# A graph network's GRU on one core: the tile of 53 rows taken last instead of ninth

## The chip, the cores and the metric

The kernel runs on 1 core of one Trainium2 chip. The metric is device time in microseconds of one execution. The median of the three runs of the kernel before is 858.27 us (856.66 to 858.71). Engine names are those of the profile: PE is TensorE (PEld its weight loads), DVE is VectorE, ACT is ScalarE, POOL is GpSimd, and SPq is the queue on which SyncE issues transfers.

## The reference, cut to what matters

3125 nodes have 256 features each; 103125 edges (with loops) join them. A layer norm and three graph convolutions come first and give `x` anew. The second half is one relational step whose result goes through a GRU cell, node by node:

```python
h = jnp.maximum(_layernorm(x, axis=-1), 0.0)
msg = h[edge_src] + relvectors[edge_rel]
red = jax.ops.segment_sum(msg, edge_dst, num_segments=h.shape[0])
gi = red @ w_ih.T + b_ih              # 3125 x 768
gh = h @ w_hh.T + b_hh
r = sigmoid(i_r + h_r); z = sigmoid(i_z + h_z)
n = tanh(i_n + r * h_n)
x = x + (1.0 - z) * n + z * h
```

## The kernel before, in words

The nodes are cut into T = 25 tiles of 128 rows, of which the last, tile 24 (`T - 1`), holds only 53 (`TAIL`). The edges are turned once into a matrix of counts, `count`, which stays on chip, so that every sum over neighbours is a row of dense f16 matmuls. All engines' programs are written by hand, instruction by instruction, and joined by semaphores; nothing reorders them. What an engine executes, and in which order, is the order of the Python calls.

The last stage is the relational sum with the GRU. The sum for the 24 full tiles is made in three parts, p = 0, 1 and 2, of eight tiles each (tiles 0 to 7, 8 to 15, 16 to 23), by a scheme with seven products in place of eight for each part. The sum for tile 24 is made apart, by `rest_pe` during p = 0, and is kept in `rest_sum`, a place in SBUF of its own, until the GRU takes it. While PE makes the products of part p, it puts the GRU of the eight or nine tiles of part p - 1 between them; the GRU of part 2 stands after all products. `gru_order` says which tile the GRU takes as its nth, and `gru_before(p)` how many tiles it takes before those of part p. The tail of PE's program for one part reads, in `paired_sums_next_pe` (n is `gru_before(p - 1)`):

```python
            product_pe(p, T3, every, False, nothing).then_inc(product_done, 1)
            for g in range(n + 6, gru_before(p) - 1):
                gru_pe(g)
            last_tail_pe(p)
            gru_pe(gru_before(p) - 1)
```

`product_pe` is line L1744 of the profile and `last_tail_pe` two matmuls at L1752. DVE's program has the same form: it adds up the blocks of a sum (`block_dve`, L1898) between its tiles of the GRU.

One tile of the GRU is, on PE (`gru_tile_pe`): input to the r and z gates (L757), state to the r and z gates (L764), state to the n gate (L769), input to the n gate (L774), all in f32 with 256 features in two halves. DVE and ACT follow (`gru_tile_dve`, L790 to L809; `gru_tile_act`, L706 to L735): bias, sigmoid, tanh, and the mix with the state and the residual. L790 waits for the matmuls of L764, and L809 makes the result.

The transposed state of a tile, which the matmuls of L764 and L769 take as stationary operand, is read from DRAM (`state_scratch`) into one of two places. SP issues these loads, the stores of the results and the loads of `x1` in one queue:

```python
            if stored and i + 2 < T:
                SP.wait_ge(nh_done, i + 1)
                state_load_sp(order, i + 2)
            SP.wait_ge(result, i + 1)
            SP.dma_start(out[t * P:t * P + rows(t), :], ...)
            if i + AHEAD < T:
                gru_load_sp(order, i + AHEAD)
```

A full tile's state takes 4 transfers of 32 KB (L664), the short one's takes 8 of 8 KB. `nh_done` is counted when L769 of the tile is through, so the state of a tile is asked for when the tile two before it has let go of the place. The store of a result is L692, the load of `x1` L668.

Of the kernel before, what the change touches and what calls it, by code (L numbers as in the profile page):

```python
# [53 lines left out]
def program(nc, x, src, dst, rel, convs, relvec, w_ih_t, w_hh_t, b_ih, b_hh, x1_dram, table_dram, mixed_dram, second_dram, h_dram, out):  # L54
# [3 lines left out]
    T = -(-N // P)  # L58
# [24 lines left out]
    with ExitStack() as ctx:  # L83
# [1347 lines left out]
        def layers_pe():  # L1431
# [42 lines left out]
            for n in range(gru_before(2), T):  # L1474
                gru_pe(n)
# [7 lines left out]

        gru_order = [*range(0, 8), T - 1, *range(8, T - 1)]
        first_sum, rest_sum = far_stage.rearrange("p c a d -> p (c a d)").bitcast(F32), pair_b[:, 0:2, :]
        block_sums = [(agg[:, 0, :], agg[:, 1, :], *(weight[f].rearrange("p f d -> p (f d)") for f in range(2))),
                      tuple(block_sums_b)]
# [1 line left out]

        def gru_before(p):

            return 8 * p + 1 if p else 0

        def columns_of(p, half):
            return slice(p * FREED + half * CHUNK, p * FREED + (half + 1) * CHUNK)
# [322 lines left out]
        def paired_sums_next_pe(p):  # L1820

            n, every = gru_before(p - 1), range(PAIRED)
            if p > 1:
                PE.wait_ge(*block_out_at(p - 1, "c21"))
# [28 lines left out]
            for g in range(n + 6, gru_before(p) - 1):  # L1853
                gru_pe(g)
# [778 lines left out]
```

## Time and profile before

| | us |
|---|---|
| median of three runs | 858.27 |
| the profiled execution's own time | 857.42 |
| its span | 853.2 |
| PE busy in the span | 821.6 (96%) |
| DVE busy | 606.7 (71%) |
| ACT busy | 297.6 (35%) |

The span is from the first to the last recorded event of the execution; its own time is 4.22 us more. A term of a sum is made against 857.42. The GRU's tiles run from 658 us to the end.

### The profile page before, as it was taken

To read this page: it belongs to the slowest core of one execution; us is meant where nothing else is said; L and a number is where in the kernel's file an instruction comes from. 1 tells how busy PE (TensorE), PEld (TensorE's weight loads), DVE (VectorE), ACT (ScalarE), POOL (GpSimd) and SP (SyncE) were. 2 spreads that over 40 slices of the span, in tenths; PEclk is the share of its full clock that TensorE was granted. 3 is DMA by queue.
4 is the path that set the end of the run, shared out by engine and by line. 5 is a ranking of instruction groups with operands and counts; after the bars stand their busy time and mean duration, and the time that the engine had idled before them with its cause. 6 is when DMAs were issued, how large, how long until landed. Compare 5 with 4: busy or idle time off the path is not lost.

```text
span 853.2 us, 14286 instructions
## 1 busy us (share of the span) xinstructions
PE 821.6 (96%) x4710; PEld 465.7 (55%) x4710; DVE 606.7 (71%) x1319; ACT 297.6 (35%) x604; POOL 123.8 (15%) x244
## 2 busy tenths in 40 slices
PE   2889999999999999999999999999999999999997
PEld 1457566666666545445555544555554555455554
DVE  8955999999999265555867546575665656565677
ACT  3365666776777312110101302221202122112233
POOL 0210112013000036655760000000000000000000
PEclk9989999999999999999999999999999999999999
DMA  6100000000000511613301112222704112112232
GB/s 208 33 2 1 4 18 23 16 17 18 24 17 17 171 30 51 183 41 76 76 8 49 59 50 98 87 75 84 201 23 145 38 42 51 28 37 44 56 81 52
DMA packets 89689, 49.83 MB, mean 58 GB/s; under 512 B 52843, under 2 KB 86396, under 8 KB 89612
## 3 DMA queue, kind: packets, MB, share of 16 engines
q1 hardware_dynamic: 73836, 39.00, 16.3%
q10 hardware_dynamic: 15776, 9.85, 4.1%
q8 instruction: 42, 0.69, 0.3%
q14 instruction: 35, 0.29, 0.1%
HBM read 29.68 MB, written 18.78 MB: 57 GB/s over the span
## 4 chain that ended last, share of the span: by engine, by line
PE 89%; DVE 7%; issue 1%; ACT 1%; DMA 1%; SPq 0%; DVEq 0%
PE ps L1396 19%; PE ps L1058 13%; PE ps L1744 11%; PE ps L955 9%; PE ps L1570 9%; PE ps L757 5%; PE ps L764 5%; PE ps L1421 4%; PE ps L1439 3%; PE ps L769 2%; PE ps L774 2%; PE ps L1030 2%; PE ps L986 1%; DVE node_b L298 1%; PE ps L1018 1%
## 5 line engine op out<-in xcount | busy, mean ns | idle before, releaser
L1058 PE MATMUL ps<-node_a,count 128*128 128x512 f16 x525 | 181.0, 381 | 1.5 <-DVE node_a L1165 1.1
L955 PE MATMUL ps<-node_b 128*128 128x175 f16 x808 | 162.2, 256 | 5.5 <-DVE node_b L298 3.5
L298 DVE TENSOR_TENSOR node_b<-node_b 128x1024 f16<-128x1024 f16 (+2 forms) x253 | 157.1, 669 | 0.0
L1254 ACT ACTIVATE count<-ps 128x500 f32 x202 | 122.9, 608 | 65.1 <-PE ps L955 59.4
L1396 PE MATMUL ps<-count,node_a 128*128 128x512 f16 (+2 forms) x686 | 130.7, 351 | 0.0
L2329 POOL TENSOR_TENSOR count<-count,node_a 16x20 f16 x202 | 89.7, 444 | 94.9 <-DMA chapter_starts<-in_dst 53.9
L955 PEld LDWEIGHTS ps<-node_b 128*128 128x128 f16 x808 | 79.5, 100 | 35.0 <-issue 7.0
L1396 PEld LDWEIGHTS ps<-count,node_a 128*128 128x128 f16 (+1 forms) x686 | 60.1, 98 | 69.1 <-issue 0.4
L1744 PE MATMUL ps<-count,node_a 128*128 128x512 f16 x288 | 64.1, 379 | 0.0
L1058 PEld LDWEIGHTS ps<-node_a,count 128*128 128x128 f16 x525 | 53.2, 101 | 18.9 <-ACT count L1254 1.2
L727 ACT ACTIVATE count<-count 128x512 f32<-128x512 f32 (+1 forms) x25 | 15.8, 630 | 118.3 <-DVE count L790 118.3
L1570 PE MATMUL ps<-count,node_b 128*128 128x512 f16 x240 | 52.9, 379 | 0.7 <-issue 0.7
L1069 POOL TENSOR_TENSOR count<-count,ident 128x128 f16<-128x128 f16 x21 | 24.2, 1151 | 185.5 <-ACT count L1254 185.5
L1702 DVE TENSOR_TENSOR count<-count 128x6144 f16<-128x6144 f16 x14 | 47.0, 3355 | 5.0 <-PE ps L1570 4.4
L1744 PE MATMUL ps<-count,node_b 128*128 128x512 f16 x216 | 47.6, 379 | 0.1
L764 PE MATMUL ps<-count,node_b 128*128 128x512 f32 (+1 forms) x100 | 47.0, 592 | 0.0
L1396 PE MATMUL ps<-count,node_b 128*128 128x512 f16 (+3 forms) x300 | 46.2, 314 | 0.0
L1744 PEld LDWEIGHTS ps<-count,node_a 128*128 128x128 f16 x288 | 28.1, 98 | 33.0
L2115 ACT ACTIVATE agg<-ps,scales 128x512 f32<-128x512 f32 (+1 forms) x20 | 12.1, 608 | 86.2 <-PE ps L1421 52.1
L790 DVE TENSOR_TENSOR count<-ps,count 128x512 f32<-128x512 f32 (+1 forms) x25 | 17.3, 691 | 32.7 <-PE ps L764 32.6
L1570 PEld LDWEIGHTS ps<-count,node_b 128*128 128x128 f16 x240 | 23.4, 98 | 28.9 <-issue 1.1
L966 PE MATMUL ps<-node_b 128*128 128x25 f16 x201 | 38.9, 194 | 0.0
(289 smaller groups left out, 1134.0 us busy)
## 6 DMA issues: line engine op xcount, KB each, us to landing
node_a<-in_x SPq DMA_DIRECT2D x4, 768.0 KB, 8.2
second_scratch<-node_a ACTq DMA_DIRECT2D x4, 768.0 KB, 3.8
node_a<-second_scratch ACTq DMA_DIRECT2D x4, 768.0 KB, 4.3
node_b<-second_scratch ACTq DMA_DIRECT2D x8, 384.0 KB, 5.1
state_scratch<-params SPq DMA_DIRECT2D x24, 128.0 KB, 1.9
node_b<-state_scratch SPq DMA_DIRECT2D x96, 32.0 KB, 2.1
table_scratch<-agg SPq DMA_DIRECT2D x21, 128.0 KB, 1.8
mixed_scratch<-node_b SPq DMA_DIRECT2D x10, 256.0 KB, 2.0
```

The costliest lines, as they stand in the source:

```text
L298: return DVE.tensor_tensor(to, iota, keys.unsqueeze(2).to_broadcast([P, n, width, 2]), ALU.is_equal)
L757: PE.matmul(ps[0:m, rz, 0:2 * D], sums[f], w_ih_rz[:, f, :], start=(f == 0), stop=False)
L764: done = PE.matmul(ps[0:m, rz, 0:2 * D], hs[f], w_hh_rz[:, f, :], start=False, stop=(f == HALVES - 1))
L955: return PE.matmul(window(s)[:, :, keys], low, key_hot[k][:, j, :, i].rearrange("p (t w) -> p t w", w=SPAN), start=(s == 0 and j == 0), st ...
L966: PE.matmul(window(s + 1)[:, :, 0], low, carry_hot[s // GROUP % 2][:, s % GROUP // 2, :, i], start=True, stop=False, skip_group_check=True)
L1058: last = PE.matmul(out_slot(u)[0:m, :], count[:, t, u * P:u * P + m], node_a[:, t, :, :].rearrange("p a d -> p (a d)"), start=(t == 0), st ...
L1254: ACTE.activation(to, window(s), ACT.Copy).then_inc(win_written, 1)
L1396: done = PE.matmul(ps[:, b, 0:cols], nodes[0:k, t, part, f * P:(f + 1) * P], count[0:k, t, c * CHUNK:c * CHUNK + cols], start=(first and n ...
L1570: done = PE.matmul(to, second_table(p, which, i, part), count[:, 2 * i + odd, columns_of(p, half)], start=(start and i == 0 and part == 0) ...
L1702: DVE.tensor_tensor(to, to, of, op).then_inc(step_made, 1)
L1744: done = PE.matmul(ps[:, bank_of(p, which), :], table_of(which, i, part), count[:, 2 * i + odd, columns_of(p, half)], start=(start and n = ...
L2329: POOL.tensor_tensor(to, to, chapter_counts[chapter % 2][:, at_place // GROUP, at_place % GROUP, :], ALU.add).then_inc(rel_placed, 1)
```

## The change

The GRU takes the tiles in plain order, 0 to 24. The short tile, until now the ninth (after tiles 0 to 7, and so at the end of the products of part 1), becomes the twenty-fifth and last, and the GRU has 8, 8 and 9 tiles after parts 0, 1 and 2 where it had 9, 8 and 8. No work is added or removed: each engine has as many instructions as before.

```diff
-        gru_order = [*range(0, 8), T - 1, *range(8, T - 1)]
+        gru_order = [*range(T)]
...
         def gru_before(p):
 
-            return 8 * p + 1 if p else 0
+            return 8 * p
```

On PE this is how the end of the products of part 1 reads before the change. The first two rows end the GRU of tile 7, L1752 is `last_tail_pe(1)`, the rows with 53 are the short tile, and L1744 are the first 72 matmuls of part 2.

```order
L774 MATMUL ps<-count,params 128x256
L774 MATMUL ps<-count,agg 128x256
L1752 MATMUL ps<-count,node_b 128x512 x2
L757 MATMUL ps<-count,node_b 53x512 x2
L764 MATMUL ps<-count,node_b 53x512 x2
L769 MATMUL ps<-count,node_b 53x256 x2
L774 MATMUL ps<-count,node_b 53x256 x2
L1744 MATMUL ps<-count,node_b 128x512 x72
```

And this is the same place on PE with the change; the rows between L1752 and L1744 are now tile 7.

```order
L1752 MATMUL ps<-count,node_b 128x512 x2
L757 MATMUL ps<-count,params 128x512
L757 MATMUL ps<-count,agg 128x512
L764 MATMUL ps<-count,node_b 128x512 x2
L769 MATMUL ps<-count,node_b 128x256 x2
L774 MATMUL ps<-count,params 128x256
L774 MATMUL ps<-count,agg 128x256
L1744 MATMUL ps<-count,node_b 128x512 x72
```

The short tile has left this place, and `last_tail_pe(1)` stands one tile of the GRU nearer to the products of T3 that are ahead of it, as it does in part 2 in both kernels.

On SP's queue the kernel's last transfers before the change are these (state of tile 23, result of tile 21, then the last two results):

```order
L692 DMA out<-pair_a 128x256
L668 DMA xt<-x_scratch 128x256
L664 DMA node_b<-state_scratch 32x8x32 x4
L692 DMA out<-pair_a 128x256
L692 DMA out<-count 128x256
L692 DMA out<-pair_a 128x256
L2526 UNCONDITIONAL_BRANCH
```

With the change the same seven rows, where tile 24 is the last, read so:

```order
L692 DMA out<-pair_a 128x256
L668 DMA xt<-x_scratch 53x256
L664 DMA node_b<-state_scratch 32x2x32 x8
L692 DMA out<-pair_a 128x256
L692 DMA out<-count 128x256
L692 DMA out<-pair_a 53x256
L2526 UNCONDITIONAL_BRANCH
```

The last result is one of 53 rows, and the last load of a state is one of 8 transfers where it was one of 4.

## Rows read from the trace of the kernel before

**Rows 1.** The page's head and its first line of busy times.
```profile
span 853.2 us, 14286 instructions
PE 821.6 (96%) x4710; PEld 465.7 (55%) x4710; DVE 606.7 (71%) x1319; ACT 297.6 (35%) x604; POOL 123.8 (15%) x244
```

**Rows 2.** Three stretches: us; busy PE, PEld, DVE, ACT, POOL; clock, DMA share, GB/s.
```profile
658.44:727.57 69.13, 69.13 (x249) 36.31 (x247) 43.82 (x84) 16.52 (x34) 0.00 (x0) 1.00 0.19 44
727.57:801.71 74.14, 74.14 (x290) 38.61 (x290) 41.55 (x74) 14.55 (x30) 0.00 (x0) 1.00 0.16 37
801.71:848.16 46.45, 46.45 (x145) 27.16 (x143) 35.46 (x82) 16.85 (x35) 0.00 (x0) 1.00 0.29 69
```

**Rows 3.** Timeline of PE around the short tile: start us, us, instruction.
```profile
721.75 0.60 PE L1752 MATMUL ps<-count,node_b 112*128 112x512 f16 x2
722.27 1.92 PE L757 MATMUL ps<-count,node_b 128*53 128x512 f32 x4
724.03 1.88 PE L764 MATMUL ps<-count,node_b 128*53 128x512 f32 x4
...
727.57 15.71 PE L1744 MATMUL ps<-count,node_b 128*128 128x512 f16 x72
```

**Rows 4.** Timeline of PE, a full tile between the same two neighbours.
```profile
743.12 0.60 PE L1752 MATMUL ps<-count,node_b 112*128 112x512 f16 x2
...
748.72 5.34 PE L1744 MATMUL ps<-count,node_a 128*128 128x512 f16 x24
```

**Rows 5.** Timeline of PE, the last two tiles.
```profile
837.83 1.02 PE L757 MATMUL ps<-count,params 128*128 128x512 f32 x2
...
842.99 1.02 PE L757 MATMUL ps<-count,params 128*128 128x512 f32 x2
...
844.70 1.88 PE L764 MATMUL ps<-count,node_b 128*128 128x512 f32 x4
```

**Rows 6.** Timeline of DVE and SP's queue after the last full tile.
```profile
846.62 0.69 DVE L790 TENSOR_TENSOR count<-ps,count 128x512 f32<-128x512 f32 x1 [0.77 <-PE ps L764]
...
850.58 0.42 DVE L809 TENSOR_TENSOR pair_a<-pair_a 128x256 f32<-128x256 f32 x1
851.03 0.33 SPq L692 DMA_DIRECT2D out<-pair_a  x1
```

**Rows 7.** The same timeline after the short tile.
```profile
725.95 0.68 DVE L790 TENSOR_TENSOR count<-ps,count 53x512 f32<-53x512 f32 x1 [0.68 <-PE ps L764]
...
729.87 0.42 DVE L809 TENSOR_TENSOR count<-count,pair_a 53x256 f32<-53x256 f32 x1
730.31 0.28 SPq L692 DMA_DIRECT2D out<-count  x1
```

**Rows 8.** The same for the stretch of the last store.
```profile
851.80:852.40 0.60, 0.00 (x0) 0.00 (x0) 0.00 (x0) 0.00 (x0) 0.00 (x0) 0.50 0.65 213
```

**Rows 9.** Transfers: the last store, then all 25 stores (L692), issue to landing.
```profile
out<-pair_a SPq DMA_DIRECT2D x1, 128.0 KB, 2.1
...
DMA to landing us min/median/max: 1.7/1.7/3.2
```

**Rows 10.** Loads of states on SP's queue: the short tile's, and the last full one's.
```profile
715.92 3.61 SPq L664 DMA_DIRECT2D node_b<-state_scratch  x8
...
837.16 2.53 SPq L664 DMA_DIRECT2D node_b<-state_scratch  x4
```

**Rows 11.** Landing of these: the short tile's eight, then all 104 of L664.
```profile
node_b<-state_scratch SPq DMA_DIRECT2D x8, 8.0 KB, 1.6
...
L664 SPq DMA_DIRECT2D node_b<-state_scratch x104: 325/612/1089, 644.3 to 839.1; - x104
...
DMA to landing us min/median/max: 1.5/2.1/4.4
```

**Rows 12.** Timeline of part 2's end: block sum after T3, then last_tail_pe.
```profile
796.31 0.75 DVE L1898 SCALAR_TENSOR_TENSOR params<-ps,scales,node_b 128x512 f32<-128x512 f32 x1 [2.53 <-PE ps L1744]
...
801.27 0.60 PE L1752 MATMUL ps<-count,node_b 112*128 112x512 f16 x2
```

## The prediction

> **What bounds the kernel now.** I read the page first: PE is busy for 821.6 of 853.2 us [rows 1]. That is a mean over the whole kernel, so I then asked for the busy times of the stretches in which the GRU runs. From the first tile of the GRU to the end of the last one PE is busy in every one of the 69.13, 74.14 and 46.45 us, at a granted clock of 1.00, which is the upper of its two levels (2.4 GHz). DVE is busy for 43.82, 41.55 and 35.46 us of the same stretches and ACT for 16.85 at most [rows 2]. So from 658.44 to 848.16 us the time is PE's work, and it does not matter in which order PE does it, unless an order makes PE wait. What is not PE's work stands behind it: after the last matmuls of L764 DVE and ACT still have the whole of a tile's gates to do, and then the result is stored. This drain begins at 846.62 and ends with the span at 853.2 [rows 1, 6], 6.58 us. The change can act in three ways only: on what the short tile costs PE, on the drain, and by a new wait.
>
> The sum is made against the profiled execution: span 853.2, own time 857.42, so 4.22 us lie outside the span. The median of the runs shown is 858.27, 0.85 us above it.
>
> **PE's part.** The short tile has 53 columns of stationary operand in place of 128, but its moving operands are as wide as a full tile's. From the start of `last_tail_pe(1)` ahead of it to the first product behind it are 727.57 - 721.75 = 5.82 us [rows 3]. The same piece with a full tile in it takes 748.72 - 743.12 = 5.60 us [rows 4]. So the short tile is no cheaper for PE than a full one; it costs 0.22 us more, in two places. A full tile takes 842.99 - 837.83 = 5.16 us [rows 5], so `last_tail_pe` ahead of it takes 5.60 - 5.16 = 0.44. The short tile's L757 begins 722.27 - 721.75 = 0.52 after it, 0.08 later than that, and goes on to L764 in 724.03 - 722.27 = 1.76 us, where the last full tile takes 844.70 - 842.99 = 1.71 [rows 3, 5], 0.05 more. The other 0.09 us lie at the end, where PE returns to 128 columns. These look like weight loads that are not hidden where the shape changes. Put last, the short tile still pays the first two (0.13), since they stand ahead of its L764, and not the third, since no matmul of 128 columns follows. This term is **-0.09 us**.
>
> All else on PE only changes place. Between `last_tail_pe(1)` and the products of part 2 stands a full tile now, 7, as in part 2 it does before. Everything from there on to the end of tile 23 comes 5.16 + 0.22 = 5.38 us earlier, and the last tile gives back 5.16 + 0.13 = 5.29, which is the -0.09 again.
>
> **The drain, DVE and ACT.** From the start of L790 to the issue of the store are 851.03 - 846.62 = 4.41 us for the last full tile [rows 6] and 730.31 - 725.95 = 4.36 us for the short one [rows 7]. Fewer partitions make these instructions no shorter: L790 takes 0.69 on 128 rows and 0.68 on 53. The term is **-0.05 us**.
>
> **The last store.** Issued at 851.03, it lands 2.1 us later [rows 6, 9], and the span ends 2.17 us after the issue. In the stretch from 851.80 to 852.40 the chip moves 213 GB/s for 0.60 us, which is 128 KB, the store itself [rows 8]. At that rate the 53 KB of the short tile take 54272 / 213e9 = 0.25 us in place of 131072 / 213e9 = 0.62, so 0.36 us less. This is an upper bound for an orderly case, since the first and the last bytes do not come at that rate; the lower bound is nothing, for the other stores of 128 KB land in 1.7 us in the median [rows 9], which shows that 0.4 us of a landing can come and go for reasons other than size. Together, 0.36 and that 0.4 bound it from above at 0.8. I take **-0.30 us**, near what the rate gives, since the last store has no other traffic beside it.
>
> The Trainium skill, on its page "DMA: Bandwidth & Descriptors", section "Anatomy of one DMA", puts a transfer at a fixed part of about 2.0 us, most of it the receipt of the write, and a variable part of its bytes over 436 GB/s. By that rule the 75 KB less are worth an estimated 0.18 us, and the whole sum would be 0.32 us where mine is 0.44. The trace agrees that most of the 2.1 us do not depend on the bytes (0.60 us of it moves them), but not with a constant, since other stores of the same size landed in 1.7.
>
> **What the change moves on SP.** The short tile's state is loaded with 8 transfers, 3.61 us of SP's queue, where a full tile's 4 take 2.53 [rows 10]. Now they are the last load, asked for when L769 of tile 22 is through. Before, the last load started at 837.16 and the matmuls of L764 that want it at 844.70: 7.54 us, and 7.67 with the 0.13 above. 3.61 of issue and 1.6 of landing [rows 10, 11] are 5.21, which leaves 2.46 us. Behind these transfers in SP's queue waits the store of tile 22, for which nobody waits, and the two last stores come 5 and 10 us later. They were asked for in just this rhythm of full tiles before, at 715.92, and PE took the short tile with none but the 0.08 us of delay. This edit costs nothing, and up to the 2.46 us it stays so.
>
> **What is moved on DVE and ACT at the end of part 1.** `last_tail_pe(1)` waits for the block sum of T3 on DVE. It stood two tiles of PE's work behind T3, and now one. In part 2 it stood one tile behind already: the block sum starts at 796.31, takes 0.75, and `last_tail_pe` starts at 801.27 [rows 12], so 4.21 us of cover are left. The block sum c22 (L1898, 0.75 us each) now stands ahead of tile 7 rather than of the short tile; it is the order of part 2. This costs nothing; without the cover it would be 0.75 us once.
>
> **Sum.** -0.09 - 0.05 - 0.30 = -0.44 us, so 857.42 - 0.44 = 856.98 for an execution like the profiled one, and 858.27 - 0.44 = 857.83 beside the median. A new measurement is a median too, and I forecast **857.8**.
>
> **The rivals.**
>
> A late state, slower. Mechanism: the 8 transfers of the last state, in the densest part of the GRU, land after PE wants them, and PE waits at L764 of the last tile, with nothing behind it to fill the gap. It decides once issue and landing take over 7.67 us. With the longest landing of the trace, 4.4 us [rows 11], they take 3.61 + 4.4 = 8.01, 0.34 late, still not to be measured. If all eight issues took the longest 1.09 us too [rows 11], they would take 8 x 1.09 + 4.4 = 13.12, 5.45 late, and the time would be 857.83 + 5.45 = 863.3. For it speaks a DMA share of 0.29 there against 0.19 in the first stretch [rows 2]; against it, that the same eight took 3.61 and 1.6 before. Chance 3%.
>
> A drain that shrinks with the rows, faster. If a tile of 53 rows went through the gates in 53/128 of the time, 4.41 x 75/128 = 2.58 us would go, and 2.97 with the 0.30 of the store and the 0.09 of PE, so 858.27 - 2.97 = 855.3. The rows of the two tiles, 4.41 and 4.36 us, are against it [rows 6, 7]. Chance 1%.
>
> No gain at the store. Its landing is the round trip, and a store that is shorter ends no sooner: 858.27 - 0.14 = 858.1. For it speaks the spread between 1.7 and 2.1 at one size. Chance 20%. By the skill's rule above it would be an estimated 857.95, between this and the forecast.
>
> My forecast has 73%; 3% are left for what I have not seen, such as another wait at the end of part 1, on either side.
>
> **How the numbers follow.** The three runs before lie between 856.66 and 858.71, so about 0.3% (2.6 us) is what a measurement can tell from no change. All of my sum, and its bounds from -0.14 to -0.94, lie well within that. The range takes the lowest run with the largest gain, 856.66 - 0.94 = 855.7, made 856.0 since both at once are unlikely in a median, and reaches up to 859.8: the highest run without a gain, 858.71 - 0.14 = 858.6, and about as much again as the runs differ from their median (0.4 to 1.6), for a chip on another day. Faster by over 0.3%: 3% (the shrinking drain, half of the unseen, chance of the measurement); slower: 4% (the late state, and the rest); within: 93%.
>
> **What would show it.** In the profile after: PE busy without idle time from the first tile to the last; L1744 of part 2 starting about 5.4 us sooner than 727.57; the last L790 on 53 rows starting at 846.53; 4.36 us from there to the last store, and less than 2.17 from that to the end; a span near 852.8. I am wrong if PE idles ahead of the last L764, if the last load of a state takes over 7 us, or if `last_tail_pe(1)` waits for DVE.

## The result

The changed kernel takes 859.84 us in the median of 11 runs (858.52 to 860.68), the kernel before 857.63 (856.56 to 858.71) beside it. The ratio is 1.0025, with a 95% interval from 1.0017 to 1.0033, so the change makes it slower by 1.5 to 2.8 us. The forecast was 857.8 with a range from 856.0 to 859.8. The direction was wrong, and the time lies just outside the range.

The profiled execution of the changed kernel took 858.70 us with a span of 854.7, against 857.42 and 853.2 before. These are the stretches of the GRU that answer to [rows 2], columns as there:

```profile
658.64:721.95 63.31, 63.31 (x232) 34.22 (x231) 39.84 (x75) 14.46 (x30) 0.00 (x0) 1.00 0.19 44
721.95:796.07 74.12, 74.12 (x290) 38.60 (x289) 41.70 (x74) 14.64 (x30) 0.00 (x0) 1.00 0.16 38
796.07:847.82 51.75, 51.75 (x161) 29.16 (x159) 39.37 (x91) 18.92 (x39) 0.00 (x0) 1.00 0.29 67
```

PE is busy throughout, at the full clock, as before. One tile has moved from the first stretch to the last. Nothing inside the GRU was lost. The timeline of PE around the last tiles, to be held against [rows 3, 5]:

```profile
721.51 0.59 PE L774 MATMUL ps<-count,agg 128*128 128x256 f32 x2
721.95 15.70 PE L1744 MATMUL ps<-count,node_b 128*128 128x512 f16 x72
...
837.35 1.02 PE L757 MATMUL ps<-count,params 128*128 128x512 f32 x2
...
842.60 1.92 PE L757 MATMUL ps<-count,node_b 128*53 128x512 f32 x4
844.36 1.88 PE L764 MATMUL ps<-count,node_b 128*53 128x512 f32 x4
```

Part 2 starts at 721.95 where it was 727.57. From the L757 of tile 23 to that of the short tile behind it are 842.60 - 837.35 = 5.25 us, and from there to its L764 844.36 - 842.60 = 1.76, against 5.16 and 1.71 with a full tile in the last place. What follows is the drain, the timeline of DVE and of SP's queue that answers to [rows 6, 7]:

```profile
846.28 0.68 DVE L790 TENSOR_TENSOR count<-ps,count 53x512 f32<-53x512 f32 x1 [0.91 <-PE ps L764]
...
850.19 0.42 DVE L809 TENSOR_TENSOR pair_a<-pair_a 53x256 f32<-53x256 f32 x1
850.63 0.26 SPq L692 DMA_DIRECT2D out<-pair_a  x1
```

The last store is issued at 850.63, 0.40 us earlier than before. But the span ends at 854.7, 4.07 us after that issue, where it was 2.17: with a last store of 53 KB the end comes 1.9 us later than with one of 128 KB. The windows after the issue (columns as in [rows 8]) say how:

```profile
851.60:853.80 2.20, 0.00 (x0) 0.00 (x0) 0.00 (x0) 0.00 (x0) 0.00 (x0) 0.50 0.08 21
853.80:854.70 0.90, 0.00 (x0) 0.00 (x0) 0.00 (x0) 0.00 (x0) 0.00 (x0) 0.50 0.07 22
```

The 128 KB moved at 213 GB/s with 0.65 of the 16 DMA engines busy [rows 8]. The 53 KB move at 21 to 22 GB/s with a share of 0.07 to 0.08, and one engine of 16 is 0.0625. The little above it belongs to another queue (q14): the view of transfers from 851.60 to 853.80 gives the queue of the store (columns: packets, MB, share of the 16 engines)

```profile
q1 hardware_dynamic: 38, 0.04, 6.3%
```

It looks as if one engine writes all rows, one after another.

The differences add up to the span's. From the first L757 of the GRU (658.64, before 658.88) to the last L790 it is 187.64 us against 187.74, -0.10; from there to the store 4.35 against 4.41, -0.06; from the store to the end 4.07 against 2.17, +1.90. That is +1.74 us, and the GRU began 0.24 earlier in this execution, which leaves +1.5. The +1.74 lies in the interval of the timed runs, 1.5 to 2.8. The medians differ by more, 2.2 us; the last section shows why.

### The profile page after: what moved, and what is told of

Read it like the earlier page. It is cut to its first block, busy times and chain, and to the rows that moved or that the text cites. A ratio compares the mean times of both kernels' runs of the same rounds, so it can differ in the third digit from the quotient of the medians.

```text
span 854.7 us, 14286 instructions
## 1 busy us (share of the span) xinstructions
PE 820.6 (96%) x4710; PEld 465.0 (54%) x4710; DVE 606.6 (71%) x1319; ACT 297.4 (35%) x604; POOL 121.9 (14%) x244
## 4 chain that ended last, share of the span: by engine, by line
PE 89%; DVE 7%; issue 1%; ACT 1%; DMA 1%; SPq 0%; DVEq 0%
PE ps L1396 19%; PE ps L1058 13%; PE ps L1744 11%; PE ps L955 9%; PE ps L1570 9%; PE ps L757 5%; PE ps L764 5%; PE ps L1421 4%; PE ps L1439 3%; PE ps L774 2%; PE ps L769 2%; PE ps L1030 2%; PE ps L986 1%; DVE node_b L298 1%; PE ps L998 1%
## 5 line engine op out<-in xcount | busy, mean ns | idle before, releaser
L1744 PE MATMUL ps<-count,node_a 128*128 128x512 f16 x288 | 64.1, 379 | 0.0
L1069 POOL TENSOR_TENSOR count<-count,ident 128x128 f16<-128x128 f16 x21 | 21.9, 1045 | 187.6 <-ACT count L1254 187.6
L1744 PE MATMUL ps<-count,node_b 128*128 128x512 f16 x216 | 47.6, 379 | 0.1
L764 PE MATMUL ps<-count,node_b 128*128 128x512 f32 (+1 forms) x100 | 47.0, 592 | 0.0
L1744 PEld LDWEIGHTS ps<-count,node_a 128*128 128x128 f16 x288 | 28.1, 98 | 33.1
L790 DVE TENSOR_TENSOR count<-ps,count 128x512 f32<-128x512 f32 (+1 forms) x25 | 17.3, 690 | 32.7 <-PE ps L764 32.6
```

Of the source, the lines that this page charges most:

```text
L764: done = PE.matmul(ps[0:m, rz, 0:2 * D], hs[f], w_hh_rz[:, f, :], start=False, stop=(f == HALVES - 1))
L1744: done = PE.matmul(ps[:, bank_of(p, which), :], table_of(which, i, part), count[:, 2 * i + odd, columns_of(p, half)], start=(start and n = ...
```

## The experiments

The theory of the first four was the one engine; the rivals were the place of the short tile with the new division into 8, 8 and 9 tiles, and a last store that lands late whatever its form.

**The last store in 48 and 5 rows.** On top of the changed kernel:

```diff
-            SP.dma_start(out[t * P:t * P + rows(t), :], h_tile[slot][0:rows(t), :]).then_inc(out_done[slot], 16)
+            cuts = (0, 48, 53) if stored and i == T - 1 else (0, rows(t))
+            for r0, r1 in zip(cuts, cuts[1:]):
+                SP.dma_start(out[t * P + r0:t * P + r1, :], h_tile[slot][r0:r1, :]).then_inc(out_done[slot], 16)
...
```

The lines left out make SP's wait at the end count one store more, here and wherever a store is cut below.

> The changed kernel with its last store, 53 rows, cut into one of 48 rows and one of 5. Theory: a store's rows are dealt over the 16 DMA engines only where their number has a common factor with it that allows it; 53 is prime, so one engine writes all 53 rows one after another, about 2.87 us / 53 = 54 ns each. Cut, the 48 go 3 to an engine and the 5 take 0.27 us, after 0.35 us of a second issue: from the first issue to the end of the span 1.8 to 2.2 us in place of 4.07, so the time 1.9 to 2.3 us below the changed kernel's and within 0.5 of the kernel before (ratio 0.9995 to 1.0003). Rival 1, the place of the short tile or the new division of 8, 8 and 9 tiles costs the time: the ratio stays at 1.0025. Rival 2, a last store lands late whatever its size or form: from its issue to the end stays 4 us.

It took 857.13 us, ratio to the kernel before 1.0005 (0.9996 to 1.0015). SP's queue at its end:

```profile
850.75 0.71 SPq L694 DMA_DIRECT2D out<-pair_a  x2
```

The span is 853.0, so 2.25 us from the first issue to the end in place of 4.07. As far as can be measured the whole loss is gone with this one edit, with the order of the change left as it is. Place and division are not the cause, and a last store is not late as such.

**The short tile second last.** On top of the changed kernel:

```diff
-        gru_order = [*range(T)]
+        gru_order = [*range(T - 2), T - 1, T - 2]
```

> The changed kernel with the short tile second last (tiles 0 to 22, 24, 23), so 8, 8 and 9 tiles as in the change, and a last store of 128 rows. Theory of the one engine: the short store's slow landing is covered by the last tile's 5.16 us, the end is that of the kernel before: last store to end 2.17 us, ratio 1.0000 within 0.0005. Rival 1, place or division costs: ratio 1.0020 to 1.0025.

It took 858.35 us, ratio 1.0010 (1.0001 to 1.0019). That is above what I expected, though the interval takes in my upper bound of 1.0005. Its profiled execution took 856.96 us with a span of 853.1, and SP's queue reads:

```profile
845.61 0.28 SPq L692 DMA_DIRECT2D out<-count  x1
851.01 0.34 SPq L692 DMA_DIRECT2D out<-pair_a  x1
```

The last store is issued at 851.01 (before: 851.03) and the end is 2.1 us later. The profile thus shows an end like that of the kernel before; the short store, issued at 845.61, has 7.5 us. Most of the 0.1% in the timed runs goes with the granted clock: 6 of its 11 executions had a mean clock of 0.991, and 7 of the 27 of the kernel before. At 0.991 the medians are 858.65 and 858.30, at 0.995 (3 and 14 executions) 856.96 and 856.72. What is left, 0.2 to 0.4 us, is not explained.

**127 rows and 1 in the kernel before.** The last store, of 128 rows, with `cuts = (0, 127, 128)`.

> The kernel before with its last store, 128 rows, cut into one of 127 rows and one of 1. Theory of the one engine: 127 is prime too, so 127 rows run on one engine, 127 x 54 ns = 6.9 us, and from the first issue to the end are 1.2 + 6.9 + 0.05 = 8.1 us in place of 2.17: slower by 5.9 us, ratio 1.0069. Rival 1 (place or division): no more than a second issue, 0.3 us, ratio 1.0004. Rival 2 (whatever comes last lands late): the same, 1.0004.

It took 862.55 us in four executions, ratio 1.0059 (1.0043 to 1.0074). SP's queue, and the window of the transfer:

```profile
851.60 1.60 SPq L694 DMA_DIRECT2D out<-pair_a  x2
```

```profile
853.00:858.00 5.00, 0.00 (x0) 0.00 (x0) 0.00 (x0) 0.00 (x0) 0.00 (x0) 0.50 0.08 25
```

The span is 859.0: 7.4 us from issue to end, with the same share of 0.08 at 25 GB/s (6.7% of it the queue of the store). The single row waited behind the 127: these 5 us hold only packets of 1 KB, and the two short packets that belong to the two stores come behind them, from 858.0 to 858.5 (the short packets are explained with the table below). A loss of this kind appears in the old order, with a full tile, once the rows of the store are 127. It is smaller than the 8.1 us forecast, since my 54 ns a row were too many. From 53 rows in 4.07 us and 128 rows in 7.4 follow (7.4 - 4.07) / 75 = 44 ns for each row of 1 KB, 23 GB/s, and 4.07 - 53 x 0.044 = 1.7 us that do not depend on the rows.

**51 rows and 2.** The changed kernel with `cuts = (0, 51, 53)`.

> The changed kernel with its last store cut into 51 rows and 2. If the number of engines is the largest divisor of the rows up to 16, 51 = 3 x 17 rows go to 3 engines, 17 x 54 ns = 0.92 us: from the first issue to the end about 2.1 to 2.3 us, some 1.9 below the changed kernel. If only multiples of 16 are dealt out and all else goes to one engine, 51 x 54 ns = 2.75 us and 3.95 to 4.1 us to the end, the same as the changed kernel (ratio 1.0025).

It took 857.47 us, ratio 1.0003 (0.9994 to 1.0012). Queue and window:

```profile
851.01 0.60 SPq L694 DMA_DIRECT2D out<-pair_a  x2
```

```profile
851.80:852.60 0.80, 0.00 (x0) 0.00 (x0) 0.00 (x0) 0.00 (x0) 0.00 (x0) 0.50 0.19 51
```

The span is 853.4, so 2.39 us to the end. The DMA share is 0.19, which is three engines of 16 (0.1875). 17 rows each make 1.7 + 17 x 0.044 = 2.45. So it is not that only multiples of 16 are dealt out: 51 rows, which 3 divides, go over three engines.

**120 rows and 8 in the kernel before.** `cuts = (0, 120, 128)`, the same number of stores as with 127 and 1.

> The kernel before with its last store, 128 rows, cut into one of 120 rows and one of 8: two stores, as with 127 and 1. If the number of engines is the largest divisor of the rows up to 16, 120 rows go to 15 engines, 8 each, and the 8 rows to 8 engines, 0.34 us later: first issue to end 2.1 to 2.4 us, ratio 1.0000 within 0.0008. If only multiples of 16 are dealt out, 120 rows run on one engine, and 1.68 + 120 x 0.045 = 7.1 us are needed, ratio 1.0057. It also prices the cut itself, which the run with 127 and 1 had in it.

It took 857.49 us, ratio 1.0002 (0.9993 to 1.0012). The queue and the window:

```profile
851.21 0.70 SPq L694 DMA_DIRECT2D out<-pair_a  x2
```

```profile
852.00:852.60 0.60, 0.00 (x0) 0.00 (x0) 0.00 (x0) 0.00 (x0) 0.00 (x0) 0.50 0.77 201
```

The span is 853.5, 2.29 us to the end, at 201 GB/s. A cut costs 0.1 us here (2.29 against 2.17), and 120 rows, no multiple of 16, are not slow.

**The load of the short tile's x1 in 48 and 5 rows.** Its store is left alone:

```diff
-            SP.dma_start(x1_tile[i % AHEAD][0:rows(t), :], x1_dram[t * P:t * P + rows(t), :]).then_inc(x1_in[i % AHEAD], 16)
+            cuts = (0, 48, 53) if order is gru_order and t == T - 1 else (0, rows(t))
+            for r0, r1 in zip(cuts, cuts[1:]):
+                SP.dma_start(x1_tile[i % AHEAD][r0:r1, :], x1_dram[t * P + r0:t * P + r1, :]).then_inc(x1_in[i % AHEAD], 16)
...
```

The part left out is ACT's wait for x1, which counts one transfer more.

> The changed kernel with the load of the short tile's x1 (53 rows, L668) cut into 48 and 5, the store left alone. Theory of the one engine: ACT's L706 of the short tile waited 0.98 us for this load in the changed kernel; cut, it lands 2 us sooner and that wait is gone, but since L727 behind it still had 1.06 us of idle time, the time stays that of the changed kernel: ratio 1.0025, last store to end 4.0 to 4.1 us. Rival: the load is what costs the 2 us, ratio 1.0000.

It took 858.73 us, ratio 1.0016 (1.0007 to 1.0025), in which interval both the changed kernel's 1.0025 and the +1.74 us of its trace (1.0020) lie, and 1.0000 does not. Its median is 1.1 us below the changed kernel's, but not at a like clock: at 0.994 its six executions took 858.5 to 858.8 us and the changed kernel's three 858.5 to 858.7. In the changed kernel the timeline of ACT showed a wait for this load:

```profile
838.65 0.42 ACT L735 ACTIVATE pair_a<-pair_a 128x256 f32<-128x256 f32 x1 [1.03 <-DVE pair_a L800]
840.05 0.60 ACT L706 ACTIVATE pair_a<-xt,negmr,rstd 53x256 f32<-53x256 f32 x1 [0.98 <-DMA xt<-x_scratch]
841.71 0.63 ACT L727 ACTIVATE count<-count 128x512 f32<-128x512 f32 x1 [1.06 <-DVE count L790]
```

With the load cut, where L706 has become L708 and L735 L737, and SP's last store stands under them:

```profile
839.94 0.42 ACT L737 ACTIVATE pair_a<-pair_a 128x256 f32<-128x256 f32 x1 [1.03 <-DVE pair_a L802]
840.26 0.59 ACT L708 ACTIVATE pair_a<-xt,negmr,rstd 53x256 f32<-53x256 f32 x1
```

```profile
851.91 0.26 SPq L694 DMA_DIRECT2D out<-pair_a  x1
```

The wait is gone, and the end still comes 4.1 us after the store (span 856.0). In the changed kernel the load was issued at 835.47 and ACT could start 4.58 us later, where the landings of L668 that the view gives have a median of 2.1. That fits one engine for the load too; its engines were not read apart, since the state's transfers ran beside it. The load was 1.06 us from costing something: that much idle time stood behind it on ACT.

**52 rows by SP and 1 by ACT.** The changed kernel with a last store of 52 rows, and at the end of ACT's program:

```diff
+            ACTE.wait_ge(result, T)
+            ACTE.dma_start(out[N - 1:N, :], h_tile[(T - 1) % AHEAD][TAIL - 1:TAIL, :]).then_inc(out_done[(T - 1) % AHEAD], 16)
```

> The changed kernel with its last store in two that are issued at once: 52 rows by SP (52 = 4 x 13, so 13 engines with 4 rows each) and the last row by ACT, which is through by then. First issue to end 1.68 + 4 x 0.045 = 1.9 us, where the cut into 48 and 5 on SP alone took 2.25, and the chain ahead of it is 0.14 us shorter than in the kernel before: 0.4 us below the kernel before, ratio 0.9995, too little to be told from 1. Should ACT's issue be slower than SP's, it ends like the cut into 48 and 5.

It took 857.55 us, ratio 1.0001 (0.9992 to 1.0010). Both transfers are issued together:

```profile
852.01 0.34 SPq L694 DMA_DIRECT2D out<-pair_a  x1
852.01 0.49 ACTq L2198 DMA_DIRECT2D out<-pair_a  x1
```

The span is 854.0, so 2.0 us from issue to end, the shortest of all and 0.2 below the kernel before. In the time it can't be told from the kernel before, as expected. No version tried beats it by what can be measured.

## Why the prediction was wrong

**The step that failed** is "The last store": the term of -0.30 us measured +1.90. I took the rate of a transfer of 128 rows, 213 GB/s, and let 53 rows run at it, as if only the bytes counted. The runs show that the number of rows decides over how many engines they are dealt: 53 and 127 over one, 51 over three, 120 and 128 over about all.

The traces hold a count that says the same without any rate. Each row is a packet of 1 KB, and some packets under 512 B come with every store. Here is the line of packets from the last store on, for 53 rows, for 48 and 5, and for 51 and 2 (packets under 2 KB are the 53 rows and the short ones):

```profile
DMA packets 57, 0.08 MB, mean 19 GB/s; under 512 B 1, under 2 KB 54, under 8 KB 54
DMA packets 80, 0.10 MB, mean 10 GB/s; under 512 B 21, under 2 KB 74, under 8 KB 74
DMA packets 64, 0.10 MB, mean 10 GB/s; under 512 B 5, under 2 KB 58, under 8 KB 58
```

These are 1, 21 and 5 short packets, and the largest divisors up to 16 are 1 for 53, 16 + 5 for 48 and 5, and 3 + 2 for 51 and 2. In all seven cases of the table below the count is that sum. So the 5 rows went over five engines, where my expectation for that run had put them on one.

The ends go by 1.7 us and 44 ns for each row of the busiest engine, to within 0.2 us (a second issue on SP comes 0.35 us after the first):

| last store | short packets | rows on the busiest engine | 1.7 + rows x 0.044 | issue to end, us |
|---|---|---|---|---|
| 128 rows (before) | 16 | 8 | 2.05 | 2.17 |
| 53 rows (changed) | 1 | 53 | 4.03 | 4.07 |
| 48, then 5 | 21 | 3, then 1 | 2.09 with 0.35 | 2.25 |
| 51, then 2 | 5 | 17 | 2.45 | 2.39 |
| 127, then 1 | 2 | 128 | 7.33 | 7.4 |
| 120, then 8 | 23 | 8, then 1 | 2.09 with 0.35 | 2.29 |
| 52 and 1 at once | 14 | 4 | 1.88 | 2.0 |

The cases of 53 and of 127 rows fixed the two numbers; the other five did not. The 0.16 and 0.2 us of the two stores with 0.35 in their sum are not explained. That these are numbers of engines is read from the share of busy time, the divisors and the short packets; no row names an engine.

The Trainium skill has the rule, on the same page that the prediction drew on ("DMA: Bandwidth & Descriptors"), in the section "Why a DMA increments its semaphore by 16 and not by 1": a transfer is split over the largest number up to 16 that divides the outermost dimension of both its sides, and 127 rows get one engine. The traces agree in every case above (for 53: 22 GB/s where 128 rows had 213). That page of the Trainium skill gives the rule of 2.0 us and 436 GB/s, which the prediction held beside its own term, for transfers issued by GpSimd; this store is issued by SP. By that rule 53 KB would land in an estimated 2.1 us, and 4.07 passed to the end.

**The bound that left no place for a loss.** I bounded the store's term by "nothing" from below, so the loss had no place in the range, and the rivals had no mechanism for it. The trace of before had this very store. Here are windows of it, 2.3 to 3.3 and 4.1 to 5.1 us after its issue at 730.31 [rows 7], when no transfer of 128 rows is left from that time:

```profile
732.60:733.60 1.00, 1.00 (x6) 0.44 (x5) 0.00 (x0) 0.64 (x2) 0.00 (x0) 1.00 0.05 17
734.40:734.60 0.20, 0.20 (x3) 0.10 (x1) 0.00 (x0) 0.00 (x0) 0.00 (x0) 1.00 0.07 26
734.60:735.40 0.80, 0.80 (x6) 0.34 (x4) 0.00 (x0) 0.00 (x0) 0.00 (x0) 1.00 0.00 0
```

Something still ran there at one engine's share and stopped by 734.60, at most 4.3 us after the issue: the late end was to be read before the change. The landings of [rows 9] could not show it. They cover only the 17 stores out of `pair_a`; for the 8 out of `count`, the short tile's among them, the view gives no landing. I had read how long the short tile's instructions take on PE and DVE, but for its store I had only the time of its issue, and put the rate of another transfer in the place of its landing.

**What held.** PE: -0.09 forecast for PE, -0.10 measured. DVE and ACT: -0.05 forecast, -0.06 measured. Part 2 starts 5.62 us sooner than before, 0.24 of it because the GRU began sooner, which leaves the 5.38 of the prediction. The load of the last state: eight transfers in 3.61 us, as before, and no wait at L764; the rival of the late state did not come. The end of part 1: no wait at `last_tail_pe(1)`, which ran from 716.35 to the L757 at 716.78, 0.43 us. The drain did not shrink with the rows. All my signs of error, an idle PE, a late state, a waiting `last_tail_pe`, lay ahead of the store, and none of them appeared. Of what was to show the forecast right, "less than 2.17" us from the last store to the end failed, with 4.07. I had overlooked the load of x1 on SP, which is the same kind of transfer and came within 1.06 us of mattering.

**Size against sign.** The 1.74 us of the trace are 0.20%, within the 0.3% that I called "no change"; with 11 runs the measurement tells it from nothing.

## What to carry to other kernels

Look at the number of rows of whatever transfer ends a kernel, or ends a wait: a remainder tile such as this one of 53 rows, a number that nothing from 2 to 16 divides, is slower to store than a full one. It wants a full tile behind it, or a cut (48 and 5), whose end is 0.1 us later than a full tile's. When work is moved to the end, time its transfers from issue to landing where they now stand, and do not carry over the rate of a larger one. A cover that hides a slow store in the middle is gone at the end.

## What the runs showed of the hardware

The clock early in the kernel differs between executions of the same program. Up to the last load, the changed kernel and the one with the cut load are the same instructions; here are the stretches 25 to 75 us of the first, and then of the second (granted clock third from the right):

```profile
25.00:50.00 25.00, 21.10 (x92) 9.66 (x90) 23.36 (x73) 10.79 (x28) 7.62 (x12) 0.93 0.06 12
50.00:75.00 25.00, 21.36 (x150) 16.26 (x149) 12.38 (x38) 15.27 (x39) 0.39 (x1) 0.93 0.01 1
```

```profile
25.00:50.00 25.00, 20.55 (x88) 9.45 (x86) 23.34 (x73) 10.15 (x26) 7.62 (x12) 0.86 0.06 13
50.00:75.00 25.00, 21.80 (x145) 16.42 (x145) 11.14 (x36) 14.92 (x39) 0.39 (x1) 0.86 0.01 1
```

At 0.86 in both stretches in place of 0.93, more of the time was spent at the lower level (1.2 GHz), and the last store was issued at 851.91 rather than 850.63, 1.28 us later. The first L757 of the GRU already starts 659.92 - 658.64 = 1.28 us later, so the difference arose before the GRU. That is as much as a change of this size, which is why the issue-to-end times above tell more than the medians.

The times of all executions go with the clock in the same way. Of 27 executions of the kernel before, taken beside the first four experiments, 14 had a mean granted clock of 0.995 and took 856.2 to 857.5 us, and 7 had 0.991 and took 858.1 to 859.2. Of the changed kernel's eleven, 3 had 0.994 (858.5 to 858.7) and 7 had 0.990 (859.5 to 860.7). The 0.001 between the kernels is about what the longer end at the lower level makes of the mean (an estimate: 1.9 us x 0.5 / 855 us). At like clock the medians of these runs, taken apart in time, differ by 858.70 - 856.72 = 2.0 and by 860.04 - 858.30 = 1.7 us. That is nearer to the 1.74 of the traces than the 2.2 between the medians of the result. What makes an execution one or the other was not tried.
